# Folding the value bias of a cross-attention into its output bias, and evicting the value projections on another engine

## The chip, the cores and the metric

The kernel runs on one core of a Trainium2 chip, as one program. The metric is the device time in microseconds. The kernel before takes 440.7 us, the median of three runs (440.47 to 440.99). Its engines are TensorE (PE; its weight loads are listed apart as PEld), VectorE (DVE), ScalarE (ACT), GpSimd (POOL) and SyncE (SP), which issues most of the transfers.

## The reference

The input x has 8 batches of 112 rows of 256 columns; a context has 8 batches of 375 rows. One decoder layer, all in float32:

```python
x = layernorm(x + self_attention(x))            # 16 heads of 64
x = layernorm(x + cross_attention(x, ctx, mask))  # 16 heads of 16
x = layernorm(x + experts(x))                   # 8 routed experts of 512, and a shared one

# cross-attention
q = split(query @ Wq.T + bq); k = split(ctx @ Wk.T + bk); v = split(ctx @ Wv.T + bv)
probs = softmax(where(mask == 0, -1e10, q @ k.T * scale))
out = merge(probs @ v) @ Wo.T + bo
```

The rows of `probs` add up to 1. So `merge(probs @ (v0 + bv))` is `merge(probs @ v0) + bv`, and the output is `merge(probs @ v0) @ Wo.T + (bo + bv @ Wo.T)`.

## The kernel before

The program has three stages. An order written out by hand, engine by engine, sets what follows what; semaphores carry the dependencies. Each engine runs its list strictly in order.

Stage 1 is the self-attention, one batch after another (`for b in range(B)` in each engine's block). TensorE's order in a batch is: scores of the first head pair, the output product `out1(b - 2)`, projections of later batches (`between1`), second scores, transposes (`turn`), value products (`value1`). VectorE takes row maxima, normalises, evicts the transposes and the Q/K projections (`evac_qk`) and does the layernorm; ScalarE does the exponentials. At the end of batch 1 come a few small steps that prepare the cross-attention. After `value1(1, 1)` TensorE does one product into bank 7 (L596, `q_any`). VectorE, in `query_scale` (L1155), waits for it, computes `parity` (L1159) and two halves of `qscale` (L1162), and with that releases `prep` 7, for which TensorE waits in `out1(0)` (L500) right after the first scores of batch 2. In VectorE's list the row maxima of batch 2 stand behind `query_scale`. In batches 6 and 7 of this stage TensorE also projects the keys and values of batch 0 of the cross-attention; VectorE evicts those three value tiles (`evac_v`, L1179).

Stage 2 is the cross-attention. Its work is cut into 32 slots: slot n is batch b = n // 4 and group g = n % 4 of four heads, one head in each row strip of the array. In slot n TensorE does `score2(n)` (L600), four score strips into banks 0 to 3; transposes the probabilities of slot n - 1 in four parts (`turn2_`); does the value product of slot n - 2 (`value2`); and between these, at places 0, 1 and 2 of the slot (`between`, L699), projections, transposes and output products. VectorE masks each strip and takes its maximum (`mask_and_max`), evicts the last of the four transposes (`evac_pt2`), and at its own places does queries, values and layernorms. ScalarE computes the exponentials (`exps2`, one a strip), evicts three of the four transposes (`evac_pt`), and the keys, x1T and x2T, partly in `before_exps` and `between`.

The value projection of a batch has three tiles of 125 context rows and 256 columns. TensorE writes tile 2 of batch b at place 1 of group 0 of that batch, and tiles 0 and 1 of batch b + 1 at place 1 of groups 2 and 3 (L706, L732, L736). All three use bank 2 (`PE_L2`), which is also the bank of score strip 2. So `lent_banks_back` (L741) makes the next slot's `score2` wait for `v_sb`, the count of evicted tiles; group 1 of a batch asks for tile 2, group 3 for tile 0 of the next batch, group 0 for tile 1. VectorE does the eviction and adds bv on the way (L1181), at place 3 of the slot, behind the fourth mask-and-maximum and `evac_pt2`: 3 tiles for batch 0 in stage 1, and 21 in stage 2.

bv is loaded as a row broadcast to all 128 partitions, beside b_out and bo (`rows`, L263); bq and bk are loaded as columns (`cols`). They and the router's and the cross-attention's weights share the semaphore `w_loaded["small"]`, ten loads in all. GpSimd adds bo to the residual (`add_bo`, L361).

Stage 3 is the routing and the experts, over tiles of 128 rows.

Of the kernel before, what the change touches and what calls it, by code (L numbers as in the profile page):

```python
# [16 lines left out]
ALU = mybir.AluOpType  # L17
ACT = mybir.ActivationFunctionType
AX = mybir.AxisListType

B, S, C = 8, 112, 256
KC = C // 128
H = 16
# [4 lines left out]
KT = 3  # L28
SK = S2 // KT
D2 = C // H  # L30
# [22 lines left out]
def build(nc, a, out):  # L53
    ctx = ExitStack()
    with ctx:
        def sb(name, shape, d=F32):
            return ctx.enter_context(nc.sbuf_tensor(name, shape, d))

        def sem(name):
            return ctx.enter_context(nc.semaphore(name))  # L60
# [11 lines left out]
        xres = sb("xres", [128, NT, C])  # L72
        x2T = sb("x2T", [128, KC, T])
        wx = sb("wx", [128, 4, KC, C])
        cols = sb("cols", [128, 2, KC])
        rows = sb("rows", [128, 3, C])
        ybuf = sb("ybuf", [128, 2, C])
        stats = sb("stats", [128, 2, 6])
        mv = sb("mv", [128, 2, 2])
# [54 lines left out]
        mask0 = sb("mask0", [S, S2])  # L134
        allm = sb("allm", [S, 1])
        anym = sb("anym", [S, 1])
        anyw = oT2[0:S, :, :].rearrange("p k n -> p (k n)")[:, 0:128]
        bias = mask0

# [63 lines left out]
        ctx_loaded = sems("ctx_loaded", 2)  # L203
        prep = sem("prep")
        q_any = sem("q_any")
        v2_ones = sem("v2_ones")
        xb2 = sem("xb2")
        x1t_pe, x1t_sb, q_pe, q_sb = (sem(n) for n in ("x1t_pe", "x1t_sb", "q_pe", "q_sb"))
# [43 lines left out]
        @block.sync  # L252
        def _(sp):
            for u in range(2):
                sp.dma_start(wqk[:, u], a["wqk"][:, u]).then_inc((w_first, w_qk[0])[u], 16)
            for u in range(1, 8):
                sp.dma_start(wqk[:, 2 * u:2 * u + 2], a["wqk"][:, 2 * u:2 * u + 2]).then_inc(w_qk[u], 16)
            for c in range(2):
                sp.dma_start(wv1[:, c], a["wv1"][:, c]).then_inc(w_v[c], 16)
            sp.dma_start(xT[:, 1:], a["xT"][:, 1:]).then_inc(xT_loaded[1], 16)  # L260
            sp.dma_start(wout, a["wout"]).then_inc(w_loaded["out"], 16)
            sp.dma_start(xres[:], a["x"]).then_inc(w_loaded["x"], 16)
            for j, n in enumerate(("b_out", "bv", "bo")):  # L263
                sp.dma_start(rows[:, j, :], a[n].to_broadcast([128, C])).then_inc(w_loaded["small"], 16)
            sp.dma_start(mask_i[:], a["mask"]).then_inc(w_loaded["mask"], 16)
            sp.dma_start(cols[:, 0, :], a["bq"]).then_inc(w_loaded["small"], 16)
            sp.dma_start(cols[:, 1, :], a["bk"]).then_inc(w_loaded["small"], 16)
            sp.dma_start(routerT[:], a["router"]).then_inc(w_loaded["small"], 16)
            for j, n in enumerate(("wq", "wk", "wv", "wo")):
                sp.dma_start(wx[:, j], a[n]).then_inc(w_loaded["small"], 16)  # L270
            for p in range(2):
                sp.dma_start(ctxT[:, p], a["ctxT"][p]).then_inc(ctx_loaded[p], 16)
            sp.dma_start(ugs[:], a["ug"][E]).then_inc(w_loaded["shared"], 16)
            sp.dma_start(dns[:], a["dn"][E]).then_inc(w_loaded["shared"], 16)

            sp.wait_ge(consts, 3)
            for t in range(ROUTED_TILES):
                sp.dma_start(slots_x[t * TILE:(t + 1) * TILE, :], blank[:, 0:C]).then_inc(zeroed, 16)
            for t in range(ROUTED_TILES):
                sp.dma_start(slots_s[t * TILE:(t + 1) * TILE, :], blank[:]).then_inc(zeroed, 16)  # L280
            def load_ctx(b):
                sp.wait_ge(v_pe, (b - 2) * KT + KT)
                sp.dma_start(ctxT[:, b % 2], a["ctxT"][b]).then_inc(ctx_loaded[b % 2], 16)

            load_ctx(2)
            sp.wait_ge(wout1, NT)
            for e in range(E):
                sp.dma_start(ug[:, e], a["ug"][e]).then_inc(w_experts, 16)
                sp.dma_start(dn[:, e], a["dn"][e]).then_inc(w_experts, 16)
                if e + 3 < B:  # L290
                    load_ctx(e + 3)

            def load_tile(t):
                sp.dma_start(xs, slots_x[bass.ds(t * TILE, TILE), :]).then_inc(xs_loaded, 16)

            def load_shared(t):
                sp.dma_start(shared_r, slots_s[bass.ds(t * TILE, TILE), :]).then_inc(shared_in, 16)

            sp.wait_ge(scattered, 16 * NT)
            load_tile(0)  # L300
            sp.wait_ge(xst_pe, 1)
            load_tile(1)
            sp.wait_ge(shared_out, 16 * NT)
            load_shared(0)
            tiles = routed_tiles(sp)
            sp.wait_ge(xst_pe, 2)
            load_tile(2)
            with sp.Fori(1, tiles - 2) as t:
                sp.wait_ge(xst_pe, t + 2)
                load_tile(t + 2)  # L310
                sp.wait_ge(ids_sb, t)
                load_shared(t)
            sp.wait_ge(ids_sb, tiles - 2)
            load_shared(tiles - 2)
            sp.wait_ge(ids_sb, tiles - 1)
            load_shared(tiles - 1)
            sp.wait_ge(stored, tiles * 16)
            sp.sem_inc(pause, 1)
# [3 lines left out]
        def _(g):  # L322
# [38 lines left out]
            def add_bo(t):  # L361
                g.wait_ge(x1_done, t + 1)
                if t < 2:
                    g.wait_ge(y1, NT)
                else:
                    g.wait_ge(y2, t - 1)
                g.tensor_tensor(xb[:, t % 2], xres[:, t], rows[:, 2], ALU.add).then_inc(xb2, 1)

            add_bo(0)
            add_bo(1)  # L370
            for t in range(NT):
# [42 lines left out]
        def _(pe):  # L414
# [159 lines left out]
            for b in range(B):  # L574
                score1(0, b)
                if b >= 2:
                    out1(b - 2)
                between1(b, 0)
                if b < 2:
                    between1(b, 1)  # L580
                score1(1, b)
                if b >= 2:
                    between1(b, 1)
                turn(0, b)
                between1(b, 2)
                turn(1, b)
                between1(b, 3)
                value1(0, b)
                turn(2, b)
                between1(b, 4)  # L590
                turn(3, b)
                between1(b, 5)
                value1(1, b)
                if b == 1:
                    pe.wait_ge(prep, 5)
                    pe.matmul(PE_W1[:, 0:S], anyw, ident[0:S, 0:S], start=True, stop=True).then_inc(q_any, 1)  # L596
            out1(NT - 1)


# [326 lines left out]
        def _(act):  # L926
# [71 lines left out]
            def evac_pt(n, r):  # L998
                i = n * STRIPS + r
                act.wait_ge(turn2, i + 1)  # L1000
                if n >= 2:
                    act.wait_ge(pv2, n - 1)
                act.activation(pT2[0:SK, i % RING], PE_T2[r][0:SK, 0:KT * S].rearrange("p (k n) -> p k n", k=KT),  # L1003
                               ACT.Copy).then_inc(pt2_act, 1)

            def before_exps(n):

                b, g = n // GROUPS, n % GROUPS
                if b == 0 and g >= 2:
                    evac_x1(g + 2)  # L1010
                if g == 1 and 1 <= b < B - 1:
                    evac_k(0, b + 1)

            def between(n, place):

                b, g = n // GROUPS, n % GROUPS
                if (g, place) == (0, 0) and b == 0:
                    evac_k(1, 1)
                if (g, place) == (1, 0) and b == 0:
                    evac_x1(3)  # L1020
                if (g, place) == (1, 0) and 1 <= b < B - 1:
                    evac_k(1, b + 1)
                if (g, place) == (3, 0) and b == 0:
                    evac_x1(6)
                if (g, place) == (1, 1) and b >= 3:
                    evac_x2(b - 3)
                if (g, place) == (3, 0) and b >= 1:
                    evac_on(b - 1)

            for n in range(SLOTS):  # L1030
                before_exps(n)
# [60 lines left out]
        def _(v):  # L1092
# [61 lines left out]

            def query_scale():  # L1155

                v.wait_ge(q_any, 1)
                v.wait_ge(consts, 4)
                v.tensor_reduce(parity[:], ident[:].rearrange("p (a two d) -> p two a d", two=2, d=D2), AX.XY, ALU.add).then_inc(prep, 1)  # L1159
# [18 lines left out]

            def evac_v(t, b, M=PE_M2):  # L1179
                v.wait_ge(v_pe, b * KT + (t + 1))  # L1180
                v.tensor_tensor(v2[:, b % 2, t, :, 0:D2], M[0:SK, 0:C].rearrange("p (h d) -> p h d", h=H),  # L1181
                                rows[0:SK, 1, :].rearrange("p (h d) -> p h d", h=H), ALU.add).then_inc(v_sb, 1)

            for n in range(8):
                evac_qk(n)
# [78 lines left out]
            def between(n, place):  # L1264
# [5 lines left out]
                    ln1_b(NT - 1)  # L1270
                if (g, place) == (0, 0) and b >= 3:
                    ln2_a(b - 3)
                if (g, place) == (0, 3) and b >= 1:
                    evac_v(2, b, PE_L2)
                if (g, place) == (1, 0) and b >= 3:
                    ln2_b(b - 3)
                if (g, place) == (1, 4) and b in (2, 4):
# [4 lines left out]
                    evac_ot(b - 1)  # L1282
                if (g, place) == (2, 4) and b >= 1:
                    normalise2(b - 1)
                if (g, place) == (2, 3) and b + 1 < B:
                    evac_v(0, b + 1, PE_L2)
                if (g, place) == (3, 3) and b + 1 < B:
                    evac_v(1, b + 1, PE_L2)

            for n in range(SLOTS):  # L1290
                between(n, 0)
# [24 lines left out]
            n = [0]  # L1316
# [179 lines left out]
```

## Time and profile before

| what | value |
|---|---|
| median of the runs | 440.7 us (440.47 to 440.99) |
| the profiled execution: time | 441.44 us |
| the profiled execution: span | 439.7 us |
| mean granted clock of TensorE | 0.996 |
| TensorE matmuls busy | 415.9 us (95%) |
| TensorE weight loads busy | 296.5 us (67%) |
| VectorE busy | 245.2 us (56%) |
| ScalarE busy | 194.1 us (44%) |
| GpSimd busy | 50.5 us (11%) |

The profile is of one execution, and every time in it is counted from the start of its span. The span is what the engines' records cover; the execution's own time is a little longer. In the order of time a row gives start, duration, engine, line of the kernel, operation, the tiles written and read, the shape, and how many instructions of the same kind it merges; a bracket at the end gives how long the engine was idle before and what released it. Stage 1 runs to about 168 us, stage 2 to about 332 us.

### The profile page before, as it was taken

To read this page: it belongs to the slowest core of one execution; us is meant where nothing else is said; L and a number is where in the kernel's file an instruction comes from. 1 tells how busy PE (TensorE), PEld (TensorE's weight loads), DVE (VectorE), ACT (ScalarE), POOL (GpSimd) and SP (SyncE) were. 2 spreads that over 40 slices of the span, in tenths; PEclk is the share of its full clock that TensorE was granted. 3 is DMA by queue.
4 is the path that set the end of the run, shared out by engine and by line. 5 is a ranking of instruction groups with operands and counts; after the bars stand their busy time and mean duration, and the time that the engine had idled before them with its cause. 6 is when DMAs were issued, how large, how long until landed. Compare 5 with 4: busy or idle time off the path is not lost.

```text
span 439.7 us, 8960 instructions
## 1 busy us (share of the span) xinstructions
PE 415.9 (95%) x3125; PEld 296.5 (67%) x3126; DVE 245.2 (56%) x724; ACT 194.1 (44%) x580; POOL 50.5 (11%) x77
## 2 busy tenths in 40 slices
PE   8999999999999978999999999999989998999992
PEld 7766868788686755777776677667665474666661
DVE  1275756756566565667575666667763452234442
ACT  1163352434426445677567666667673101011110
POOL 3010010101101001000010101010100045212222
PEclk9999999999999999999999999999999999999998
DMA  8998000000000013040404040920000013122210
GB/s 255 363 388 241 1 1 1 0 1 2 1 1 0 1 37 144 1 180 1 180 2 180 12 170 13 364 92 1 1 2 1 1 49 108 46 63 68 58 44 33
DMA packets 15241, 34.22 MB, mean 78 GB/s; under 512 B 2381, under 2 KB 9150, under 8 KB 13920
## 3 DMA queue, kind: packets, MB, share of 16 engines
q1 hardware_dynamic: 13952, 30.70, 20.0%
q0 software_dynamic: 1104, 2.76, 1.8%
q8 instruction: 25, 0.41, 0.4%
q10 hardware_dynamic: 144, 0.23, 0.2%
q14 instruction: 16, 0.13, 0.1%
HBM read 27.24 MB, written 6.70 MB: 77 GB/s over the span
## 4 chain that ended last, share of the span: by engine, by line
PE 66%; issue 23%; DVE 6%; ACT 2%; SPq 1%; DMA 0%; POOLq 0%; POOL 0%; DVEq 0%; ACTq 0%
PE bank L434 9%; PE bank L635 7%; PE bank L504 6%; PE bank L448 6%; PE bank L617 4%; PE bank L880 4%; PE bank L856 4%; PE bank L532 3%; PE bank L491 3%; PE bank L862 3%; PE bank L465 3%; PE bank L526 3%; PE bank L477 3%; PE bank L651 3%; PE bank L518 1%
## 5 line engine op out<-in xcount | busy, mean ns | idle before, releaser
L1232 DVE CUSTOM_DVE_ANT_0 p<-bank,mask 112x375 f32<-112x375 f32 x128 | 62.7, 545 | 38.6 <-PE bank L617 38.6
L996 ACT ACTIVATE p<-p,nm 112x375 f32<-112x375 f32 x128 | 74.8, 609 | 6.0 <-DVE nm L1232 6.0
L635 PEld LDWEIGHTS bank<-ident,p 112*125 112x125 f32 x384 | 48.9, 187 | 22.8 <-issue 13.7
L1003 ACT ACTIVATE pT<-bank 125x336 f32<-125x336 f32 x96 | 42.8, 447 | 46.1 <-PE bank L635 46.1
L635 PE MATMUL bank<-ident,p 112*125 112x112 f32 x384 | 58.8, 286 | 0.9
L434 PE MATMUL bank<-x2T,arena 128*128 128x224 f32 x256 | 53.9, 359 | 0.0
L939 ACT ACTIVATE p<-bank,nm 112x112 f32<-112x112 f32 x128 | 43.6, 366 | 18.6 <-DVE nm L1106 18.6
L434 PEld LDWEIGHTS bank<-x2T,arena 128*128 128x128 f32 x256 | 47.4, 194 | 0.6 <-DMA x2T<-in_xT 0.4
L349 POOL TENSOR_TENSOR rstd<-veps,minus_half 128x1 f32<-128x1 f32 x14 | 7.7, 549 | 297.2 <-DVE veps L1132 297.2
L1099 DVE TENSOR_SCALAR arena<-bank 128x448 f32<-128x448 f32 x32 | 20.0, 624 | 26.5 <-PE bank L434 26.5
L617 PE MATMUL bank<-kT,qz 32*112 32x375 f32 x256 | 28.8, 517 | 3.5 <-ACT x2T L965 2.1
L1106 DVE TENSOR_REDUCE nm<-bank 112x4 f32<-112x448 f32 x32 | 19.2, 620 | 19.9 <-PE bank L465 19.9
L448 PE MATMUL bank<-arena,x2T 128*112 128x512 f32 x64 | 30.2, 602 | 0.0
L945 ACT ACTIVATE arena<-bank 128x448 f32<-128x448 f32 x16 | 8.7, 543 | 48.0 <-PE bank L491 48.0
L939 ACT ACTIVATION_READ_ACCUMULATOR p<-bank,nm 112x1 f32 x128 | 28.1, 219 | 0.0
L504 PE MATMUL bank<-arena 128*128 128x256 f32 x112 | 26.0, 385 | 1.0 <-ACT arena L945 0.6
L532 PE MATMUL bank<-wx,mid 128*125 128x256 f32 x96 | 26.5, 399 | 0.0
L790 PE MATMUL bank<-x2T,ugs 128*128 128x512 f32 (+1 forms) x64 | 25.5, 543 | 0.6 <-DVE pT L1313 0.4
L1073 ACT ACTIVATE p<-bank 128x512 f32<-128x512 f32 x9 | 5.4, 597 | 44.8 <-PE bank L856 44.8
L651 PE MATMUL bank<-pT,v 125*32 125x112 f32 x768 | 25.0, 263 | 0.0
L651 PEld LDWEIGHTS bank<-pT,v 125*32 125x32 f32 x768 | 17.3, 109 | 10.1 <-issue 7.4
L504 PEld LDWEIGHTS bank<-arena 128*128 128x128 f32 x112 | 20.7, 190 | 4.4 <-ACT arena L945 0.9
(140 smaller groups left out, 598.0 us busy)
## 6 DMA issues: line engine op xcount, KB each, us to landing
arena<-in_ug SPq DMA_DIRECT2D x8, 1024.0 KB, 5.8
arena<-in_dn SPq DMA_DIRECT2D x8, 512.0 KB, 7.7
mid<-in_ctxT SPq DMA_DIRECT2D x8, 375.0 KB, 3.1
slots_s<-blank SPq DMA_DIRECT2D x14, 128.5 KB, 3.4
arena<-in_wqk SPq DMA_DIRECT2D x7, 256.0 KB, 4.9
slots_x<-blank SPq DMA_DIRECT2D x14, 128.0 KB, 6.9
p<-slots_s SPq DMA_DIRECT2D x9, 128.5 KB, 2.1
kT<-slots_x SPq DMA_DIRECT2D x9, 128.0 KB
```

Of the source, the lines that this page charges most:

```text
L434: mm = pe.matmul(J[:, m * S_PAIR:(m + 1) * S_PAIR], wqk[:, 2 * u + m, k, :], xT[:, i, k, :], start=(k == 0), stop=(k == KC - 1))
L448: mm = pe.matmul(PE_J1[c][0:S, :], xT[:, b // 2, k, (b % 2) * S:(b % 2 + 1) * S], wv1[:, c, k, :], start=(k == 0), stop=(k == KC - 1))
L504: mm = pe.matmul(PE_W1[:, 0:C], oT1[:, k, t * TILE:(t + 1) * TILE], wout[:, k, :], start=(k == 0), stop=(k == 7))
L532: mm = pe.matmul(M[0:SK, 0:C], ctxT[:, b % 2, k, t * SK:(t + 1) * SK], wx[:, 2, k, :], start=(k == 0), stop=(k == KC - 1))
L617: mm = pe.matmul(PE_S2[r][0:S, 0:S2], qz[rows_r, b // 2 % 2, m, par, b % 2, :], kT2[rows_r, b % 2, m, :], start=True, stop=True)
L635: mm = pe.transpose(PE_T2[r][0:SK, t * S:(t + 1) * S], p2[i % RING][:, t * SK:(t + 1) * SK], ident[0:S, 0:S])
L651: mm = pe.matmul(PE_V2[VP * r:VP * r + VP, g * S:(g + 1) * S], v2[:, b % 2, t, g * STRIPS + r, :], pT2[0:SK, (n * STRIPS + r) % RING, t, : ...
L790: mm = pe.matmul(bank[2 + 2 * (n % 2) + part][:, 0:width(grp)], ugs[:, k, part * HID + m * 128:part * HID + (m + 1) * 128], x2T[:, k, grp ...
L939: e = act.activation(p1[g][:, n, :], PE_S1[g % 2][0:S, n * S:(n + 1) * S], ACT.Exp, bias=nm1[:, h:h + 1], accum_out=rs1[:, h:h + 1])
L996: act.activation(p2[i % RING], p2[i % RING], ACT.Exp, bias=nm2[:, i % H:i % H + 1], scale=-1.0).then_inc(exp2, 1)
L1003: act.activation(pT2[0:SK, i % RING], PE_T2[r][0:SK, 0:KT * S].rearrange("p (k n) -> p k n", k=KT), ACT.Copy).then_inc(pt2_act, 1)
L1232: v.tensor_tensor_reduce(p2[i % RING], PE_S2[r][0:S, 0:S2], bias[:], 1.0, 3e38, ALU.add, ALU.min, accum_out=nm2[:, i % H:i % H + 1]).then_ ...
```

## The change

The value bias no longer goes into the value tiles. It is loaded as a column (two values a partition). VectorE widens it to a 128x256 tile in the unused keys' memory (`bvw`), TensorE multiplies that by Wo into the free half of bank 7, which gives bv @ Wo.T in each of the 128 rows, and VectorE adds it to the bo row in place. These steps stand at the end of batch 1 of stage 1: the products behind `q_any` on TensorE, the widening and the add at the head of `query_scale` on VectorE. GpSimd waits for the sum before its first `add_bo`.

The evictions of the value tiles become plain copies. Those of batch 0 stay on VectorE. The 21 of batches 1 to 7 go to ScalarE, at its place 1 of the same slots: behind the third exponential and ahead of the fourth. TensorE's order in stage 2 isn't touched.

```diff
-        cols = sb("cols", [128, 2, KC])
-        rows = sb("rows", [128, 3, C])
+        cols = sb("cols", [128, 3, KC])
+        rows = sb("rows", [128, 2, C])
...
+        bvw = kT2[:, :, :, :].rearrange("p b k n -> p (b k n)")[:, 0:KC * 128].rearrange("p (k n) -> p k n", k=KC)
...
+        bv_wide, bo_more, bo_sum = sem("bv_wide"), sem("bo_more"), sem("bo_sum")
...
-            for j, n in enumerate(("b_out", "bv", "bo")):
+            for j, n in enumerate(("b_out", "bo")):
                 sp.dma_start(rows[:, j, :], a[n].to_broadcast([128, C])).then_inc(w_loaded["small"], 16)
...
             sp.dma_start(cols[:, 1, :], a["bk"]).then_inc(w_loaded["small"], 16)
+            sp.dma_start(cols[:, 2, :], a["bv"]).then_inc(w_loaded["small"], 16)
...
-                g.tensor_tensor(xb[:, t % 2], xres[:, t], rows[:, 2], ALU.add).then_inc(xb2, 1)
-
+                g.tensor_tensor(xb[:, t % 2], xres[:, t], rows[:, 1], ALU.add).then_inc(xb2, 1)
+
+            g.wait_ge(bo_sum, 1)
             add_bo(0)
...
                     pe.matmul(PE_W1[:, 0:S], anyw, ident[0:S, 0:S], start=True, stop=True).then_inc(q_any, 1)
+                    pe.wait_ge(bv_wide, 1)
+                    for k in range(KC):
+                        mm = pe.matmul(PE_W1[:, C:2 * C], bvw[:, k, :], wx[:, 3, k, :], start=(k == 0), stop=(k == KC - 1))
+                    mm.then_inc(bo_more, 1)
...
+            def evac_v2(t, b):
+                act.wait_ge(v_pe, b * KT + (t + 1))
+                act.activation(v2[:, b % 2, t, :, 0:D2], PE_L2[0:SK, 0:C].rearrange("p (h d) -> p h d", h=H),
+                               ACT.Copy).then_inc(v_sb, 1)
...
                 if (g, place) == (3, 0) and b >= 1:
                     evac_on(b - 1)
+                if (g, place) == (0, 1) and b >= 1:
+                    evac_v2(2, b)
+                if (g, place) == (2, 1) and b + 1 < B:
+                    evac_v2(0, b + 1)
+                if (g, place) == (3, 1) and b + 1 < B:
+                    evac_v2(1, b + 1)
...
             def query_scale():
 
+                v.wait_ge(w_loaded["small"], 16 * 10)
+                v.tensor_copy(bvw, cols[:, 2, :].unsqueeze(2).to_broadcast([128, KC, 128])).then_inc(bv_wide, 1)
+                v.wait_ge(bo_more, 1)
+                v.tensor_tensor(rows[:, 1], PE_W1[:, C:2 * C], rows[:, 1], ALU.add).then_inc(bo_sum, 1)
                 v.wait_ge(q_any, 1)
...
                 v.wait_ge(v_pe, b * KT + (t + 1))
-                v.tensor_tensor(v2[:, b % 2, t, :, 0:D2], M[0:SK, 0:C].rearrange("p (h d) -> p h d", h=H),
-                                rows[0:SK, 1, :].rearrange("p (h d) -> p h d", h=H), ALU.add).then_inc(v_sb, 1)
+                v.tensor_copy(v2[:, b % 2, t, :, 0:D2], M[0:SK, 0:C].rearrange("p (h d) -> p h d", h=H)).then_inc(v_sb, 1)
...
-                if (g, place) == (0, 3) and b >= 1:
-                    evac_v(2, b, PE_L2)
...
-                if (g, place) == (2, 3) and b + 1 < B:
-                    evac_v(0, b + 1, PE_L2)
-                if (g, place) == (3, 3) and b + 1 < B:
-                    evac_v(1, b + 1, PE_L2)
...
-        "bv": by_group(g["L0_xattn_bv"], 0).reshape(1, C),
+        "bv": np.ascontiguousarray(by_group(g["L0_xattn_bv"], 0).reshape(KC, 128).T),

```

## Rows read from the trace of the kernel before

**Rows 1.** Share of the span by engine, from the chain of waits that ended last.

```profile
PE 66%; issue 23%; DVE 6%; ACT 2%; SPq 1%; DMA 0%; POOLq 0%; POOL 0%; DVEq 0%; ACTq 0%
```

**Rows 2.** Stretches: start:end, length, busy us of each engine, clock, DMA share, GB/s.

```profile
240.00:260.00 20.00, 19.87 (x204) 13.99 (x202) 12.96 (x45) 12.97 (x30) 1.25 (x2) 1.00 0.28 100
```

**Rows 3.** List of waits: us in total, times, longest.

```profile
DVE p L1232 <- PE bank L617: 38.6, 29, 6.5
```

**Rows 4.** Order of time (start, duration, engine, line, op), end of batch 1.

```profile
26.52 1.43 POOL L354 TENSOR_TENSOR xb<-xres,rows 128x256 f32<-128x256 f32 x2 [21.23 <-DMA wx<-in_wo]
...
53.12 0.62 DVE L1099 TENSOR_SCALAR arena<-bank 128x448 f32<-128x448 f32 x1 [0.76 <-PE bank L434]
...
53.93 0.47 PE L596 MATMUL bank<-ident,oT 112*128 112x112 f32 x2
...
54.34 1.04 PE L465 MATMUL bank<-arena 64*112 64x112 f32 x16
54.45 0.29 DVE L1159 TENSOR_REDUCE parity<-ident 128x2 f32<-128x128 f32 x1 [0.70 <-PE bank L596]
54.77 0.81 DVE L1162 TENSOR_SCALAR qscale<-bank,parity 128x224 f32<-128x224 f32 x2
...
55.72 3.69 PE L504 MATMUL bank<-arena 128*128 128x256 f32 x16 [0.34 <-DVE qscale L1162]
```

**Rows 5.** Groups by line and shape: count, busy us, mean ns, idle before.

```profile
L996 ACT ACTIVATE p<-p,nm 112x375 f32<-112x375 f32 x128 | 74.8, 609 | 6.0 <-DVE nm L1232 6.0
...
L1181 DVE TENSOR_TENSOR v<-bank,rows 125x256 f32<-125x256 f32 x24 | 10.2, 424 | 7.2 <-PE bank L532 7.2
...
L955 ACT ACTIVATE x1T<-bank 128x256 f32<-128x256 f32 x7 | 2.7, 380 | 0.7 <-PE bank L511 0.7
...
L1145 DVE TENSOR_SCALAR mask<-mask_i 112x375 f32<-112x375 int32 x1 | 0.3, 345 | 0.0
```

**Rows 6.** Order of time, group 2 of a steady batch.

```profile
262.02 1.12 PE L532 MATMUL bank<-wx,mid 128*125 128x256 f32 x4
...
262.76 1.11 ACT L996 ACTIVATE p<-p,nm 112x375 f32<-112x375 f32 x2
...
263.07 0.78 PE L651 MATMUL bank<-pT,v 125*32 125x112 f32 x24
263.18 0.42 DVE L1181 TENSOR_TENSOR v<-bank,rows 125x256 f32<-125x256 f32 x1 [0.33 <-PE bank L532]
...
263.83 0.32 PEld L617 LDWEIGHTS bank<-kT,qz 32*112 32x112 f32 x8 [0.22 <-issue]
```

**Rows 7.** Order of time, group 3 of a steady batch, with an output product.

```profile
267.55 1.12 ACT L996 ACTIVATE p<-p,nm 112x375 f32<-112x375 f32 x2
...
268.48 0.54 PEld L651 LDWEIGHTS bank<-pT,v 125*32 125x32 f32 x24 [0.33 <-issue]
...
269.19 0.29 PEld L617 LDWEIGHTS bank<-kT,qz 32*112 32x112 f32 x8 [0.17 <-issue]
```

**Rows 8.** Order of time, group 3 of batch 0, then group 3 of batch 1.

```profile
185.06 1.11 ACT L996 ACTIVATE p<-p,nm 112x375 f32<-112x375 f32 x2
...
185.80 0.32 PEld L617 LDWEIGHTS bank<-kT,qz 32*112 32x112 f32 x8 [0.17 <-issue]
...
204.12 1.12 ACT L996 ACTIVATE p<-p,nm 112x375 f32<-112x375 f32 x2
...
204.91 0.31 PEld L617 LDWEIGHTS bank<-kT,qz 32*112 32x112 f32 x8 [0.17 <-issue]
```

**Rows 9.** Order of time, group 2 of batch 0.

```profile
179.04 1.04 PE L532 MATMUL bank<-wx,mid 128*125 128x256 f32 x4
...
180.25 0.50 DVE L1240 COPY pT<-bank 125x336 f32<-125x336 f32 x1
...
180.67 0.41 DVE L1181 TENSOR_TENSOR v<-bank,rows 125x256 f32<-125x256 f32 x1
...
181.35 0.90 PE L617 MATMUL bank<-kT,qz 32*112 32x375 f32 x8 [0.27 <-DVE v L1181]
```

## The prediction

> **What bounds the kernel now.** I read the chain of waits first, then the stretches, then the list of waits, then the order of time around each edited place. The chain is mostly TensorE's own work (66%) and its issue (23%); VectorE holds 6% and ScalarE 2% [rows 1]. In a steady stretch of the cross-attention, 20 us long, TensorE's matmuls cover 19.87 us, while VectorE and ScalarE are each busy for about 13 us at full granted clock [rows 2]. VectorE's main work there, mask and maximum, stood idle 38.6 us for scores of TensorE [rows 3]. So relief of VectorE is worth something only where TensorE itself stood behind a VectorE instruction, and the same holds for the load put on ScalarE. What is to be asked of each edit is when TensorE's next instruction may start.
>
> **The change, part by part.**
>
> *Loading.* The broadcast of bv (128 KB) becomes a 1 KB load, still one of the ten that are waited for together. The last of the ten had landed when GpSimd's first add started at 26.52 us [rows 4], and VectorE now asks for them at 53.7 us. Nothing waits, so zero. GpSimd's new wait for the summed bias is met at some 56 us, and the sum is first used behind the last layernorm of the self-attention, six batches on: zero. SP's queue keeps its number of issues.
>
> *The new bias, at the end of batch 1 of the self-attention.* Added on VectorE: a copy that widens bv (128x256), a wait for TensorE, an add (128x256). Added on TensorE: a wait for the copy and two float32 products of 128x256, each two records of the trace. In the old trace [rows 4] VectorE ends its last Q/K eviction at 53.74, TensorE ends the q_any product at 54.40 and starts the scores of batch 2 at 54.34 (starts overlap), parity starts at 54.45, the first qscale at 54.77, and out1(0), which waits for both qscale instructions, at 55.72, having stood 0.34.
> The widening copy is not in the trace. Near rows [rows 5] say 0.345 us (one input in SBUF, 375 elements) and 0.424 us (128-row add reading PSUM, 256 elements). I take the upper: ready at 54.18, seen by TensorE 0.23 us later (the lag from VectorE's end to TensorE's next load in [rows 6]: 263.60 to 263.83), so the products start at 54.38 to 54.41 where 54.34 was free. Stall at most 0.07; with the lower value none.
> Four matmul records of 128x256 take 0.92 us of TensorE (16 take 3.69 us, [rows 4]), and VectorE's reading of such a group starts 1.16 us after its start (262.02 to 263.18, [rows 6]). The add thus starts at about 54.38 + 1.14 = 55.52. Behind it in VectorE's order stand parity, both qscales and then the row maxima of batch 2. The add lasts 0.42 and the next instruction starts some 0.08 before its end (an estimate; two exponentials on ScalarE overlap by 0.11, [rows 5, 6]), so parity starts at 55.86, qscale 0.32 later at 56.18, and out1(0) 0.95 after that, at 57.13: **+1.4 us** against 55.72. The products alone would move it only to 55.38 + 0.92 = 56.30, or +0.6 us; that is the lower bound. The upper is +1.6, if add and parity don't overlap at all and the copy is late. The maxima and the exponentials of batch 2 shift by the same, and TensorE has 3.69 us of out1 and a value projection before it needs them, so they add nothing. From there on the chain is TensorE's own work, with VectorE and ScalarE parts that themselves start from it, so the shift isn't taken back.
>
> *The three value copies of batch 0.* An add with a PSUM input (0.424 us) becomes a copy of the same size. It is no longer than that and no shorter than the 0.345 of [rows 5]: between 0 and -0.24 us in all, and VectorE is not what TensorE stands for there. I take zero.
>
> *The 21 copies moved to ScalarE.* A projection sits in the bank of score strip 2, so the next slot's scores wait until it is evicted. The place in ScalarE's order is behind the third exponential. Two consecutive exponentials last 1.11 us and one lasts 0.61 [rows 5, 6], so the instruction behind starts 0.50 us after the one ahead. A 128x256 ScalarE copy of PSUM takes 0.38 us [rows 5]. Each copy then frees the bank 0.50 + 0.38 after the third exponential's start, and the scores' weight load follows 0.23 us behind.
> Seven slots (group 2 of batches 1 to 6, group 0 of batch 7) look as [rows 6]: 262.76 + 0.50 + 0.38 + 0.23 = 263.87 against 263.83 before. Before, VectorE's end at 263.60 plus 0.23 gives just that 263.83, and the load came 0.76 us behind the value product's start where the undisturbed spacing is 0.71 [rows 7]. So the bank already set the pace by 0.05 us, and now costs 0.04 more: 7 x 0.04 = **+0.28 us**.
> Group 3 of batch 0: ScalarE has an x1 copy ahead and is late, 185.06 + 0.50 + 0.38 + 0.23 = 186.17 against 185.80, **+0.37**. Group 3 of batch 1: 204.12 + 1.11 = 205.23 against 204.91, **+0.32** [rows 8].
> Group 2 of batch 0 goes the other way. There VectorE came to v only behind a query eviction, and TensorE's scores stood 0.27 for it, until 181.35. ScalarE can take it when the product ends at 180.08, and is done at 180.5. What is late next is VectorE's pT copy, 180.75 + 0.23 = 180.98 for the load and some 181.02 for the scores; **-0.30**, rounded down [rows 9].
> Group 3 of batches 2 to 6 has an output product in between: ScalarE frees the bank at 267.55 + 0.88 = 268.43, the load was at 269.19 [rows 7]: zero. Group 0 of batches 1 to 6 has a key projection between: zero. The fourth exponential comes 0.3 to 0.4 us later in each of the 21 slots; its transpose is the last of the next slot's four, so zero. Queued behind it is also the next slot's first pT copy; ScalarE, busy 12.97 of 20 us [rows 2], has room ahead of it.
> Sum here: 0.28 + 0.37 + 0.32 - 0.30 = **+0.67 us**. If ScalarE reads PSUM with a strided output 0.05 us slower, nine places add 0.45; if the spacings are that much better, 0.35 comes off and the seven slots gain what they had lost. Bounds: +0.2 to +1.1.
> The Trainium skill (ScalarE: Activation LUTs, what ACT_TABLE_LOAD costs) gives an ACTIVATE with immediate scale and bias 186 ns plus 0.833 ns per element, 399 ns for this copy, so by it nine places would cost 0.02 us more each, 0.17 us in all. The trace has 380 ns for the same width, and the sum stays with it.
>
> *Sum.* 1.4 + 0.67 = +2.07 us: the span of 439.7 becomes 441.8, and the profiled execution's 441.44 becomes 443.5. The profiled execution stands 0.74 above the median of the runs, so the median 440.7 becomes **442.7 us**. What this measurement can tell from no change is 0.2%, or 0.88 us.
>
> **Rivals.**
> *Only the products count.* The add and the evictions are covered better than I read, out1(0) shifts by 0.6 to 1.0 and the slots even out: +0.6 to +1.1, 441.3 to 441.8, say 441.6. For it: the seven slots are decided by hundredths. Against: the dependency from product to add to qscale is serial in VectorE's order.
> *ScalarE becomes the bound.* If the fourth exponential or the pT copies, later by 0.38 us, do reach TensorE in the slots where ScalarE carries k or x2T as well, say 6 to 10 of them, it costs 2.3 to 3.8 us beyond the 2.07: 445 to 446.5; all 21 slots would give 450.7. For it: ScalarE is 65% busy in the steady stretch [rows 2] and its wait for the projection now holds its queue. Against: that is 7 us free of 20, and its part of the chain is 2% [rows 1].
> *VectorE was the bound, and the change is faster.* The place is the start of the mask-and-maximum row behind each v eviction. The 21 removed instructions are worth 21 x 0.424 = 8.9 us; less 1.4 for the bias, that is 433.2 with all of them, and 438.9 if eight of them counted (3.4 - 1.4 - some 0.2). It decides from four slots on (4 x 0.424 = 1.7 us). For it: TensorE's busy rows are modelled ends and may hide that it waits. Against: VectorE itself waited for TensorE, 38.6 us before those very instructions [rows 3].
> By the Trainium skill (Perfetto Trace Analysis, identifying the most-contended engine) matmul busy time is a poor measure of the room left on TensorE and the load of weights the better one. By that, 13.99 of 20 us [rows 2] leaves TensorE near VectorE's 12.96, and relief of VectorE would pay as in this last rival. In the order of time I found TensorE waiting for v once, at 181 [rows 9], so its chance stays small.
>
> **How the numbers follow.** Chances: my forecast 0.62, only the products 0.18, ScalarE 0.13, VectorE 0.07. The forecast's own range is 0.8 (0.6 + 0.2) to 2.9: 441.5 to 443.6. The 8-in-10 range takes in most of the second case and the lower edge of the third: 441.3 to 444.5. Slower by over 0.2% (above 441.6): nearly all of the forecast (0.60), of ScalarE (0.12) and a third of the second case (0.06), 0.78. Within 0.2%: 0.15. Faster: 0.07.
>
> **What would show it.** In the changed profile: the widening copy at about 53.8 of at most 0.43 us; the four product records between q_any and the scores; out1(0) at about 57.1 instead of 55.7. Every later self-attention stamp shifted by 1.4 alike. Behind group 3 of batches 0 and 1, TensorE's scores waiting for ScalarE's v copy by 0.3 to 0.4; in the seven slots by under 0.1; the wait for v at 181 gone. I am wrong if out1(0) moves by under 1 us, if a steady batch of the cross-attention changes its length by more than 0.2, or if the ScalarE copy lasts over 0.45.

## The result and the profile after

The changed kernel takes 442.55 us, median of six runs (442.23 to 442.97); the kernel before, with runs on the same chip added, 440.59 us (440.20 to 441.60). The ratio is 1.0040, with a 95% interval of 1.0028 to 1.0052: slower by some 1.8 us (1.2 to 2.3). Forecast were 442.7 us and +2.07. The profiled execution of the changed kernel took 442.55 us with a span of 440.8, in the middle of its runs; that of the kernel before, 441.44, was one of its slower ones. So the spans differ by only 1.1 us where the medians differ by 2.0, and the comparison must be made stage by stage, from marks that both traces have.

These rows of the changed kernel's page (busy us, share, count; then shares of the chain) and of its list of waits answer to [rows 1, 3]:

```profile
PE 416.8 (95%) x3129; PEld 296.9 (67%) x3130; DVE 236.4 (54%) x705; ACT 200.2 (45%) x601; POOL 50.6 (11%) x77
...
PE 67%; issue 23%; DVE 5%; ACT 2%; SPq 1%; DMA 0%; POOLq 0%; POOL 0%; DVEq 0%; ACTq 0%
```

```profile
DVE p L1254 <- PE bank L625: 50.9, 29, 6.5
```

VectorE is relieved of 8.8 us and shows it as 12.3 us more of standing for TensorE's scores. ScalarE took on 6 us. The chain stayed TensorE's.

In order of time, the end of batch 1, which answers to [rows 4]:

```profile
52.75 0.62 DVE L1118 TENSOR_SCALAR arena<-bank 128x448 f32<-128x448 f32 x1 [0.76 <-PE bank L438]
53.29 0.28 DVE L1177 COPY kT<-cols 128x256 f32<-128x256 f32 x1
...
53.56 0.47 PE L600 MATMUL bank<-ident,oT 112*128 112x112 f32 x2
...
53.87 1.04 PE L603 MATMUL bank<-wx,kT 128*128 128x256 f32 x4
...
54.84 1.04 PE L469 MATMUL bank<-arena 64*112 64x112 f32 x16
54.95 0.42 DVE L1179 TENSOR_TENSOR rows<-bank,rows 128x256 f32<-128x256 f32 x1 [1.38 <-PE bank L603]
55.29 0.28 DVE L1182 TENSOR_REDUCE parity<-ident 128x2 f32<-128x128 f32 x1
55.60 0.81 DVE L1185 TENSOR_SCALAR qscale<-bank,parity 128x224 f32<-128x224 f32 x2
...
56.56 3.69 PE L508 MATMUL bank<-arena 128*128 128x256 f32 x16 [0.67 <-DVE qscale L1185]
```

From VectorE's last Q/K eviction to out1(0) it is 56.56 - 52.75 = 3.81 us, against 55.72 - 53.12 = 2.60: +1.21. The reader sees the new chain: the four product records, VectorE's add behind them, parity behind the add, both qscales, and TensorE having waited 0.67 us where it had waited 0.34.

Three places of the cross-attention: group 2 of batch 0 (compare [rows 9]), group 3 of batch 0 [rows 8], and group 2 of a steady batch [rows 6].

```profile
180.93 0.38 ACT L1016 ACTIVATE v<-bank 125x256 f32<-125x256 f32 x1 [0.26 <-PE bank L536]
...
181.83 0.90 PE L625 MATMUL bank<-kT,qz 32*112 32x375 f32 x8
...
185.54 0.62 ACT L1004 ACTIVATE p<-p,nm 112x375 f32<-112x375 f32 x1
...
186.04 0.40 ACT L1016 ACTIVATE v<-bank 125x256 f32<-125x256 f32 x1
186.30 0.63 ACT L1004 ACTIVATE p<-p,nm 112x375 f32<-112x375 f32 x1
186.61 0.32 PEld L625 LDWEIGHTS bank<-kT,qz 32*112 32x112 f32 x8 [0.49 <-issue]
...
242.63 0.39 ACT L1016 ACTIVATE v<-bank 125x256 f32<-125x256 f32 x1
...
243.24 0.32 PEld L625 LDWEIGHTS bank<-kT,qz 32*112 32x112 f32 x8 [0.27 <-issue]
```

ScalarE's copy starts 0.50 us after the third exponential (185.54, 186.04), ends at 186.44, and the weight load for the next scores follows 0.17 later. I laid the starts of all 32 slots' scores of both traces side by side, each taken at its first weight load and read to 0.01 us. The changed kernel enters the cross-attention 0.81 us late; the difference then moves at ten places only:

| scores of slot | behind | moved by | forecast |
|---|---|---|---|
| 3 | group 2 of batch 0 | -0.31 | -0.30 |
| 4 | group 3 of batch 0 | +0.30 | +0.37 |
| 8 | group 3 of batch 1 | +0.29 | +0.32 |
| 7, 11, 15, 19, 23, 27, 29 | group 2 of batches 1 to 6, group 0 of batch 7 | +0.02 to +0.05 each, 0.28 in all | 0.28 |

In sum +0.56 us, with 0.67 forecast. (The seven small moves add up such readings, so their sum is good to some 0.03.) Together with +1.21 that is +1.77, which agrees with the ratio. The rest of the spans' difference lies elsewhere: 0.37 us in the changed kernel's favour before the eviction at 52.75, of which more below, and 0.3 in its favour behind the cross-attention. That last part isn't followed up: from the last scores to the end of the span the twelve profiles of this study take 115.97 to 116.50 us, though no edit lies there.

### The profile page after: what moved, and what is told of

Same layout as the page of the kernel before. It is cut to its first block, busy times and chain, and to the rows that moved or that the text cites. A ratio compares the mean times of both kernels' runs of the same rounds, so it can differ in the third digit from the quotient of the medians.

```text
span 440.8 us, 8970 instructions
## 1 busy us (share of the span) xinstructions
PE 416.8 (95%) x3129; PEld 296.9 (67%) x3130; DVE 236.4 (54%) x705; ACT 200.2 (45%) x601; POOL 50.6 (11%) x77
## 4 chain that ended last, share of the span: by engine, by line
PE 67%; issue 23%; DVE 5%; ACT 2%; SPq 1%; DMA 0%; POOLq 0%; POOL 0%; DVEq 0%; ACTq 0%
PE bank L438 9%; PE bank L643 7%; PE bank L508 6%; PE bank L452 6%; PE bank L625 4%; PE bank L536 4%; PE bank L888 4%; PE bank L864 4%; PE bank L495 3%; PE bank L870 3%; PE bank L469 3%; PE bank L530 3%; PE bank L659 3%; PE bank L481 3%; PE bank L522 1%
## 5 line engine op out<-in xcount | busy, mean ns | idle before, releaser
L1004 ACT ACTIVATE p<-p,nm 112x375 f32<-112x375 f32 x128 | 77.3, 610 | 5.4 <-DVE nm L1254 5.4
```

The costliest lines, as they stand in the source:

```text
L1004: act.activation(p2[i % RING], p2[i % RING], ACT.Exp, bias=nm2[:, i % H:i % H + 1], scale=-1.0).then_inc(exp2, 1)
```

## Experiments

Every kernel ran beside the kernel before on the same chip; its median there lay between 440.5 and 440.7 us. "The slots" are the starts of the 32 scores, as above; all shifts are against the profile before, and "from +0.10 to +0.54" means at the first slot and at the last.

**1. The bias alone.** The changed kernel, with all value copies at VectorE's old places:

```diff
-                if (g, place) == (0, 1) and b >= 1:
-                    evac_v2(2, b)
...
+                if (g, place) == (0, 3) and b >= 1:
+                    evac_v(2, b, PE_L2)
```

> The bias is folded as in the changed kernel; all value tiles stay on VectorE, at their old places, as plain copies. Theory A (two independent costs: the serial bias steps of batch 1, about 1.2 us, and the later release of the score bank, about 0.6 us): out1(0) starts 1.2 us later than before, counted from VectorE's last Q/K eviction, nothing is lost in the cross-attention, and the time is 1.0 to 1.4 us above the kernel before, ratio 1.0023 to 1.0032. Theory B (the whole loss lies in ScalarE's evictions, the bias being covered by slack later): ratio 1.000 to 1.001.

Measured: 441.52 us, ratio 1.0024 (1.0010 to 1.0037). out1(0) came 1.21 us later, counted from the same eviction. The slots stay within 0.08 us from the first to the last: a plain copy in place of the add is worth nothing (24 of them at 424 ns on average, as the adds before). Theory A holds, B falls.

**2. ScalarE's evictions alone.** The kernel before, with the 21 copies on ScalarE (bv is left out of those tiles):

```diff
+                if (g, place) == (0, 1) and b >= 1:
+                    evac_v2(2, b)
...
-                if (g, place) == (0, 3) and b >= 1:
-                    evac_v(2, b, PE_L2)
```

> The 21 evictions are on ScalarE as in the changed kernel; bv is neither added to the value tiles 1 to 7 nor folded into the output bias (it is left out of them), everything else as before. Theory A: +0.5 to +0.7 us, ratio 1.0011 to 1.0016, all of it gathered between slot 2 and slot 29 of the cross-attention: -0.3 at slot 3, +0.3 each at slots 4 and 8, and 0.02 to 0.05 at each of the seven slots behind group 2 (and group 0 of batch 7). Theory B: +1.5 to +2 us, ratio 1.0035 to 1.0045. Theory C (VectorE's relief is worth something by itself): below 1.000.

Measured: 441.89 us, ratio 1.0037 (1.0023 to 1.0052), more than theory A had. The slots show why: -0.31, +0.30 and +0.34 at slots 3, 4 and 8, the small ones at 0.04 to 0.05, and at slot 11 +0.34 where the changed kernel has 0.04. There VectorE's first mask of slot 10 begins late, behind an eviction that ended in time and with its scores ready; the trace names TensorE's transposes of slot 9, while the kernel makes this mask wait for a transpose of slot 8 only, long done:

```profile
217.34 0.61 DVE L1257 COPY oT<-bank 128x448 f32<-128x448 f32 x1
...
218.26 0.55 DVE L1243 CUSTOM_DVE_ANT_0 p<-bank,mask 112x375 f32<-112x375 f32 x1 [0.31 <-PE bank L635]
```

I ran it again:

> The same kernel as the one with ScalarE's evictions alone (bv left out of the value tiles of batches 1 to 7), run again since its first execution showed a delay of 0.34 us of VectorE's first mask in slot 10 that no wait explains. Theory A: if that was of one execution, the slots gain 0.55 to 0.60 us in all as in the changed kernel, and the ratio lies at 1.0012 to 1.0025; if it belongs to the program, slot 11 shows 0.34 again and the ratio stays near 1.0035.

Measured: 441.37 us, ratio 1.0024 (1.0015 to 1.0033), and slot 11 moved by 0.34 again. So the delay belongs to that program (it shows in neither kernel of the pair nor in any other here), and what causes it stays open. The slots move by 0.92 and 0.98 us in the two executions, which is a ratio of some 1.0021: the second measurement has it within its interval, the first lies above it. Without the delay the evictions give 0.6 to 0.7 us here, in both executions.

**3. The add behind the qscales.** The changed kernel, with the products in the bank of the transposes, so that the add need not come first (the first transposes of batch 2 then wait for the add, which gives that bank back):

```diff
-                        mm = pe.matmul(PE_W1[:, C:2 * C], bvw[:, k, :], wx[:, 3, k, :], start=(k == 0), stop=(k == KC - 1))
+                        mm = pe.matmul(PE_T1[:, 0:C], bvw[:, k, :], wx[:, 3, k, :], start=(k == 0), stop=(k == KC - 1))
...
-                v.wait_ge(bo_more, 1)
-                v.tensor_tensor(rows[:, 1], PE_W1[:, C:2 * C], rows[:, 1], ALU.add).then_inc(bo_sum, 1)
...
                 last.then_inc(prep, 1)
+                v.wait_ge(bo_more, 1)
+                v.tensor_tensor(rows[:, 1], PE_T1[:, 0:C], rows[:, 1], ALU.add).then_inc(bo_sum, 1)
```

> The changed kernel, with the bias products put into another bank and VectorE's add moved behind the two qscale instructions, so that out1(0) waits for the qscales as before and not for product and add. Theory A (the serial chain product, add, parity, qscale sets out1(0)): out1(0) comes about 0.65 us earlier than in the changed kernel, some 0.55 us later than before; TensorE's 0.67 us of waiting there falls under 0.1; time 0.5 to 0.7 us below the changed kernel. Rival (only TensorE's two products count and the waiting in front of out1(0) is slack): no change against the changed kernel, within 0.2 us.

Measured: 441.44 us, ratio 1.0026 (1.0015 to 1.0036). In order of time:

```profile
52.63 0.62 DVE L1120 TENSOR_SCALAR arena<-bank 128x448 f32<-128x448 f32 x1 [0.76 <-PE bank L438]
...
53.75 1.04 PE L605 MATMUL bank<-wx,kT 128*128 128x256 f32 x4
53.95 0.29 DVE L1182 TENSOR_REDUCE parity<-ident 128x2 f32<-128x128 f32 x1 [0.50 <-PE bank L602]
54.27 0.81 DVE L1185 TENSOR_SCALAR qscale<-bank,parity 128x224 f32<-128x224 f32 x2
54.72 1.04 PE L469 MATMUL bank<-arena 64*112 64x112 f32 x16
54.99 0.41 DVE L1190 TENSOR_TENSOR rows<-bank,rows 128x256 f32<-128x256 f32 x1
55.69 1.56 PE L510 MATMUL bank<-arena 128*128 128x256 f32 x6
```

out1(0) comes 3.06 us after the eviction, 0.46 later than before and 0.75 earlier than in the changed kernel, and TensorE doesn't wait for it at all. The serial chain was the larger part of the 1.21 (0.75); the other 0.46 is left with the products on TensorE, and experiment 4 takes it away with them. The time alone would not tell experiment 3 from the changed kernel, since the intervals of their ratios overlap; the distances in the traces do.

**4. The products moved** to slot 0 of the cross-attention, the add to slot 1 (the widened bias then lies in the unused part of `oT2`, and the first value product waits for the add; these lines and those taken out at the end of batch 1 are left out below):

```diff
                     pe.wait_ge(ot1[1], B)
                     project_k(1, 1)
+                    pe.wait_ge(bv_wide, 1)
+                    pe.wait_ge(ot1[0], B)
+                    for k in range(KC):
+                        mm = pe.matmul(PE_V2[:, 0:C], bvw[:, k, :], wx[:, 3, k, :], start=(k == 0), stop=(k == KC - 1))
+                    mm.then_inc(bo_more, 1)
...
+                if n == 1 and place == 4:
+                    v.wait_ge(bo_more, 1)
+                    v.tensor_tensor(rows[:, 1], PE_V2[:, 0:C], rows[:, 1], ALU.add).then_inc(bo_sum, 1)
```

> The changed kernel, with the bias products moved to slot 0 of the cross-attention, where TensorE stands 0.9 to 1.5 us for VectorE's first maxima, and the add to VectorE's place 4 of slot 1, where it stands 1.2 us for scores; the widening copy stays in batch 1 (0.28 us). Theory A: out1(0) back within 0.3 us of the kernel before, start of slot 1 unchanged, time 1.0 to 1.3 us below the changed kernel, ratio to before 1.001 to 1.002. Rival (the products cost 0.9 us of TensorE wherever they stand): 0.2 to 0.4 us below the changed kernel only.

Measured: 440.87 us, ratio 1.0006 (0.9997 to 1.0015), just below the 1.001 to 1.002 forecast for it, of which its interval holds the lower part. out1(0) is back at 2.60 us behind the eviction, as before. The products now stand in a gap, between the key projection and the second scores, which come 3.25 us after the first ones, as they did before (171.18 - 167.93):

```profile
168.03 0.90 PE L621 MATMUL bank<-kT,qz 32*112 32x375 f32 x8
...
168.86 1.53 PE L530 MATMUL bank<-mid,wx 128*128 128x375 f32 x4
...
170.23 1.02 PE L692 MATMUL bank<-wx,oT 128*128 128x256 f32 x4
...
171.28 0.90 PE L621 MATMUL bank<-kT,qz 32*112 32x375 f32 x8
```

The rival, that the products cost TensorE's time wherever they stand, falls. What is left is ScalarE's part: the slots move from +0.10 to +0.54, by 0.44, of which -0.12 is at slot 2 (see 5).

**5. One tile on ScalarE, 20 on VectorE**, with the products moved as in 4:

```diff
+                if n == 2 and place == 1:
+                    evac_v2(0, 1)
...
+                if (g, place) == (2, 3) and b + 1 < B and b >= 1:
+                    evac_v(0, b + 1, PE_L2)
```

> The bias products stand in slot 0 and the add in slot 1 of the cross-attention, as in the moved version; of the 21 tiles only the one of slot 2 (group 2 of batch 0), where VectorE was late behind the query eviction, goes to ScalarE, the other 20 stay on VectorE at their old places as plain copies. Theory A: out1(0) as before, slot 3 starts 0.3 us earlier than before and the lead is kept to the end, so time 0.2 to 0.4 us below the kernel before, ratio 0.9991 to 0.9996 (at the edge of what can be told). Rival (bank release isn't what held slot 3): 1.000 and no lead at slot 3.

Measured: 439.90 us, ratio 0.9986 (0.9977 to 0.9995), where 0.9991 to 0.9996 was forecast. This version beats both kernels: the kernel before by 0.6 us, and the changed one by what lies between the two ratios, 0.54% or some 2.4 us. Slot 3 starts 0.30 us earlier and the lead is kept; slots 2, 4 and 7 give another 0.11, 0.03 and 0.03. The 0.11 was not expected. GpSimd's adds of the output bias now wait for the sum and begin at 175.72, while they had begun at 172.95, beside VectorE's layernorm step. First the kernel before, then this one:

```profile
172.95 1.49 POOL L367 TENSOR_TENSOR xb<-xres,rows 128x256 f32<-128x256 f32 x2
...
173.31 0.53 DVE L1140 TENSOR_SCALAR xres<-ybuf,mv,rstd 128x256 f32<-128x256 f32 x1
```

```profile
173.54 0.41 DVE L1157 TENSOR_SCALAR xres<-ybuf,mv,rstd 128x256 f32<-128x256 f32 x1
...
175.72 1.43 POOL L370 TENSOR_TENSOR xb<-xres,rows 128x256 f32<-128x256 f32 x2 [2.50 <-DVE rows L1291]
```

That step lasts 0.41 us in the three versions that wait for the sum there (4, 5 and 9) and 0.52 to 0.53 in the other nine profiles, and slot 2 comes 0.11 to 0.12 earlier in just those three.

**6. The copies one place later**, behind the fourth exponential:

```diff
-                if (g, place) == (2, 1) and b + 1 < B:
+                if (g, place) == (2, 2) and b + 1 < B:
                     evac_v2(0, b + 1)
...
                 exps2(n, 3)
+                between(n, 2)
```

> The changed kernel, with ScalarE's 21 value copies one place later, behind the fourth exponential (0.50 us later). Theory A (TensorE's next scores wait for the bank that the copy frees): the next scores come 0.5 us later at the seven slots behind group 2 (and group 0 of batch 7) and at group 3 of batches 0 and 1, 0.3 to 0.5 at group 2 of batch 0, nothing elsewhere: +4.5 to +5 us over the changed kernel, ratio to before 1.014 to 1.016. Rival (what costs is ScalarE's time as such, wherever the copy stands): no change against the changed kernel, 1.004.

Measured: 447.09 us, ratio 1.0146 (1.0131 to 1.0162), as forecast. The slots moved by +0.50 to +0.54 at each of the seven, +0.81 and +0.79 at slots 4 and 8 (0.30 and 0.29 in the changed kernel), +0.17 at slot 3 (-0.31), nothing at slots 12, 16, 20, 24 and 28, where the output product covers it: 5.45 us in all, 4.9 more than the changed kernel. Group 3 of batch 1:

```profile
206.22 1.12 ACT L1004 ACTIVATE p<-p,nm 112x375 f32<-112x375 f32 x2
...
207.22 0.40 ACT L1016 ACTIVATE v<-bank 125x256 f32<-125x256 f32 x1
207.79 0.32 PEld L625 LDWEIGHTS bank<-kT,qz 32*112 32x112 f32 x8 [0.96 <-issue]
```

So it is the moment at which the bank is freed that counts, not ScalarE's load: the work is the same in both.

**7 and 8. GpSimd's first adds.** In the profile before, VectorE's normalise of batch 0 lasted 1.06 us, while all others of its 32 took 0.62; GpSimd's two adds ran beside it:

```profile
26.52 1.43 POOL L354 TENSOR_TENSOR xb<-xres,rows 128x256 f32<-128x256 f32 x2 [21.23 <-DMA wx<-in_wo]
```

```profile
27.37 1.06 DVE L1114 TENSOR_TENSOR p<-p,rc 112x448 f32<-112x448 f32 x1
```

In the changed kernel the adds had begun at 26.02 and ended at 27.44, just as the normalise began (27.43). Two kernels move the adds of the kernel before:

```diff
             g.wait_ge(w_loaded["small"], 16 * 10)
+            g.wait_ge(scores1[2], 2)     # kernel 7
+            g.wait_ge(prep, 5)           # kernel 8, in its place
```

> The kernel before, with GpSimd's first two residual adds held until the third scores of batch 1, so that they run from 43.2 to 44.6 us, beside VectorE's normalise of that batch (two inputs in SBUF). Theory D (such a VectorE instruction starts only when GpSimd's running adds have ended): that normalise, 0.62 us elsewhere, lasts 1.2 to 1.35 us and ends 0.47 us behind GpSimd's second add; TensorE, which waits for it, comes 0.6 us later; the first batch's normalise, 1.06 us in the kernel before's profile, is back at 0.62. Time +0.1 to +0.6 us. Rival (the 1.06 us had to do with the loads running at that time, which are over by 43 us): 0.62 us and no shift.

Measured: 440.22 us, ratio 0.9990 (0.9981 to 1.0000), where +0.1 to +0.6 us was forecast. It went the other way round:

```profile
43.47 1.82 POOL L355 TENSOR_TENSOR xb<-xres,rows 128x256 f32<-128x256 f32 x2 [38.18 <-PE bank L466]
...
44.07 0.63 DVE L1115 TENSOR_TENSOR p<-p,rc 112x448 f32<-112x448 f32 x1
```

VectorE came in as the first add ended (43.47 + some 0.72) and kept its 0.63; the second add was held, and the pair took 1.82 us for 1.43. Both of my sentences for this run fall. Nothing waits for both adds. And the rival, whose 0.62 us and no shift are what VectorE shows, doesn't explain why GpSimd's second add was held when the loads were over. What fits all cases, here and in the other traces (last section), is that two such instructions exclude each other, one at a time, and the one that comes second waits.

> The kernel before, with GpSimd's first two residual adds held until VectorE has made the mask's bias (38.9 us in the old trace), when VectorE has no instruction with two SBUF inputs until 43.9. Theory D' (a VectorE and a GpSimd instruction that both need the second read of the SBUF exclude each other, one instruction at a time; in about half of the profiled executions so far the first batch's normalise met GpSimd's adds and lost 0.33 to 0.44 us, depending on when the loads land): every normalise lasts 0.62 to 0.63, GpSimd's pair 1.43 us, and the median is 0.1 to 0.4 us below the kernel before, ratio 0.9991 to 0.9998. Rival (that moment's loss is made up later): 1.000.

Measured: 440.65 us, ratio 1.0001 (0.9989 to 1.0012). All 32 normalises last 0.62 to 0.63 and the pair takes 1.41, but the interval holds both the gain forecast and none.

**9. Versions 5 and 8 together.**

> The kernel with the bias products in slot 0, one tile on ScalarE, and GpSimd's first adds held until the mask's bias is made. Theory A with D': slot 3 starts 0.4 us earlier than in the kernel before, counted from slot 0, as in the version without the held adds; the first normalise lasts 0.62; time 0.5 to 0.9 us below the kernel before, ratio 0.998 to 0.999. Rival (GpSimd's held adds now meet another VectorE instruction on the path): no better than 0.9986, with a VectorE instruction between 38 and 41 us longer than elsewhere.

Measured: 440.10 us, ratio 0.9990 (0.9981 to 0.9999), at the edge of the 0.998 to 0.999 forecast: faster than before by little, and not to be told from version 5. Its slots move from -1.23 to -1.76, the 0.5 us of version 5. No VectorE instruction between 38 and 41 us is longer than elsewhere, as the rival wanted it.

## Why the prediction was right

The time was within 0.2 us, and the two terms have the place that was given and nearly the size: both were over, by 0.19 and 0.11 us, so the sum was 2.07 and the traces show 1.77. That the time came closer than that is in part luck: the medians differ by 2.0 us where the ratio of runs side by side gives 1.8, and 440.7 + 2.07 is 442.8, not the 442.7 that I wrote.

*The bias.* Forecast +1.4, measured +1.21 (and 1.21 in experiment 1). The mechanism, product to add to parity to qscale to out1(0), is shown by experiment 3, where taking the add out of it gives 0.75 back. It shows in every profile: from VectorE's last Q/K eviction to out1(0) it is 3.81 us in the three kernels with the whole chain there (the changed one, 1 and 6), 3.06 in experiment 3, and 2.60 in all eight others. The term was over by 0.19 because the widening copy took 0.28 us and not the 0.42 that I chose, so that TensorE started the products close behind q_any, 1.12 us after the eviction's start where I had 1.26 (53.87 - 52.75); and the add came 1.08 behind the products' start where I had 1.14 (the row that I named has 1.16). The Trainium skill (VectorE: DVE Perf Modes, Mode 2x_2P) says that a float32 copy within SBUF runs at two elements a cycle; the trace has 283 ns for 256 elements a partition, against 425 ns for the add of the same width, which reads PSUM; so it agrees. Both of my bounds, 0.345 and 0.424, were too high. That nothing gave the shift back later, as forecast, holds: experiment 1 kept it to within 0.08 us through the cross-attention.

*The evictions.* Forecast +0.67, measured +0.56, place by place as in the table, and nothing at the other slots. Experiment 6 shows the cause by moving the copies by 0.50 us: against the changed kernel all ten places answer, with 0.47 to 0.52 each, and the covered ones with nothing. The small excess of the forecast is in the lag from ScalarE's end to TensorE's load, 0.17 to 0.22 us where I had 0.23 from VectorE. ScalarE's copy took 391 ns; the sum had 380, and the Trainium skill's formula (ScalarE: Activation LUTs, what ACT_TABLE_LOAD costs) gives 399, so the trace lies between the two and neither matters.

*The gain at slot 3* was 0.31, as forecast, and experiment 5 shows it with no other tile moved.

*Loading* cost nothing, as said. What I had not priced is that a shift of its landing can move GpSimd's first adds on or off a VectorE instruction, worth 0.30 to 0.44 us in a single execution. The two met in four of the twelve profiles (the kernel before, and experiments 3, 4 and 6), and TensorE felt it: from its 65th projection record to VectorE's last Q/K eviction of batch 1 those four take 25.99 to 26.13 us, and the other eight 25.69 to 25.70. That is the 0.4 us which the profile before lost ahead of the bias steps. Besides, the first 64 projection records took 12.4 to 14.0 us in the profiles of this study, with no order that follows the edits; what sets this I did not look into. So the span of one profile is not good to better than about a microsecond in this kernel, and marks inside it are.

*The rivals.* That only the products count falls by the 1.21 us, where it allowed 1.0, by the 0.56 us that the slots kept, and by experiment 3. That ScalarE becomes the bound falls by the table and by experiment 6. That VectorE was the bound falls because it only stood 12.3 us longer for scores, and because its relief moved no slot forward but slot 3.

*Slips in the working.* The upper end of the forecast's own range should have been 1.6 + 1.1 = 2.7 us, or 443.4, and not 2.9. And the top of the 8-in-10 range, 444.5, doesn't reach the third case, which began at 445. Neither changes how the result is read.

## What to carry to other kernels

A free engine is not a reason to move work to it: the eviction's price is the moment at which it frees the bank, and VectorE, standing idle at that moment, let the next scores start 0.02 to 0.3 us earlier than ScalarE, which had an exponential under way. Move the one instance where the old engine is late, and leave the others. A small preparation step costs what it adds to the serial chain (1.21 us here) if it stands ahead of something that the critical engine waits for, and nothing in a gap where that engine stands anyway.

## What the runs showed of the hardware that I had not expected

A VectorE instruction with two float32 inputs in SBUF (112x448) and a GpSimd add (128x256) exclude each other. Beside GpSimd's pair it took 1.06, 0.95, 0.98 and 0.92 us (the kernel before and those of experiments 3, 4 and 6) where 0.62 is usual, and in each its end lies 0.48 us behind the pair's (27.95 and 28.43 in the kernel before). Where VectorE came first, GpSimd's pair took 1.82, 1.76, 1.81 and 1.64 us for 1.43 (experiments 7, 2, its repeat, and 5). A VectorE instruction with one SBUF input (128x256, per-partition scalars) took 0.53 beside GpSimd's adds, and 0.41 without. The mask-and-maximum rows, which read one input in PSUM, kept their 0.55 beside them. The Trainium skill (Advanced Engine Details and Errata, VectorE Performance Modes) says that the second SBUF port of VectorE is shared with GpSimd, and that GpSimd's instructions and VectorE's in a two-port mode block each other. The traces show such blocking for an instruction of another kind, one with two inputs in SBUF; no run here tests the mode.

That a plain copy from PSUM is no faster on VectorE than an add with an SBUF operand was as forecast: both take 424 ns. Open is the delay of some 0.3 us of one VectorE instruction in both executions of the kernel of experiment 2.
